# Attention results carried to the projection's input by transfers instead of transposes; projections evacuated by ScalarE and finished by GpSimd

## What is computed

```python
x = z; y = _layernorm(x)                        # 4 x 1024 x 256
zn = layernorm(y) * ln_scale + ln_bias;  q, k, v = zn @ w_qkv
att = softmax(q @ k.T / 4)                      # per head
out = (att @ v).reshape(b, n, 256) @ w_proj + b_proj
x = x + _layernorm(y + out)
x = x + _layernorm(ffn(_layernorm(x)))
# ffn: (ln(silu(t @ sw1.T + sb1) * (t @ sw2.T + sb2))) @ sw3.T + sb3; 512 rows of image 0 are routed
```

## Time and profile before

| | |
|---|---|
| median of 3 runs | 1050.6 us (1050.59 to 1052.78) |
| the profiled execution | 1052.78 us, span 1051.0 us |
| TensorE busy | 968.4 us, 92% |
| VectorE busy | 838.5 us, 80% |
| ScalarE busy | 606.2 us, 58% |
| GpSimd busy | 281.3 us, 27% |
| transfers | 49.4 MB |
| starts of the first and the last maxima reduction | 45.6 and 899.5 us |

### The profile page before, as it was taken

How to read it: one execution, slowest core, us unless ns; L and a number is a source line. 1 busy time by engine, 2 the same in 40 slices (tenths; PEclk the granted TensorE clock), 3 DMA queues, 4 the chain that set the end, 5 groups by cost and what they waited for, 6 DMA issues and landing times.

```text
span 1051.0 us, 16569 instructions
## 1 busy us (share of the span) xinstructions
PE 968.4 (92%) x6372; PEld 388.1 (37%) x6372; DVE 838.5 (80%) x1634; ACT 606.2 (58%) x700; POOL 281.3 (27%) x418
## 2 busy tenths in 40 slices
PE   4289999999999999999999999999999999966984
PEld 3123333333334334333343343333332333235773
DVE  4287888898887988999879889889899798445765
ACT  3025667677874775767857766667666666731110
POOL 4060001101622231207804412028142020633022
PEclk9697999999999999999999999999999999997998
DMA  5905101320160103200621031003410000231001
GB/s 139 134 1 69 54 2 41 53 70 2 41 93 30 60 22 46 69 9 1 109 94 41 1 45 52 27 1 71 91 60 24 1 2 1 78 133 52 1 1 60
DMA packets 45783, 49.42 MB, mean 47 GB/s; under 512 B 8409, under 2 KB 38889, under 8 KB 45321
## 3 DMA queue, kind: packets, MB, share of 16 engines
q1 hardware_dynamic: 44360, 46.53, 19.7%
q10 hardware_dynamic: 960, 0.79, 0.7%
q0 software_dynamic: 384, 1.05, 0.3%
HBM read 13.94 MB, written 8.91 MB: 22 GB/s over the span
## 4 chain that ended last, share of the span: by engine, by line
PE 83%; DVE 9%; DMA 2%; ACT 2%; issue 2%; POOL 1%; SPq 0%; ACTq 0%; DVEq 0%; POOLq 0%
PE obank L909 23%; PE sc L895 20%; PE ring L877 16%; PE ring L792 10%; PE ring L814 5%; DVE mx L1123 4%; PE sc L984 3%; PE ring L784 3%; PE ring L935 2%; DVE st L1059 2%; ACT prob L720 1%; DMA kp<-parts 1%; PE ring L929 1%; DMA qp<-mp 1%; DMA x_sb<-x 0%
## 5 line engine op out<-in xcount | busy, mean ns | idle before, releaser
L1123 DVE TENSOR_REDUCE mx<-ring 128x1 f32<-128x512 f32 x1024 | 635.1, 681 | 88.0 <-PE ring L877 86.3
L720 ACT ACTIVATE prob<-sc 128x1024 f32<-128x1024 f32 x512 | 495.9, 1021 | 205.4 <-PE sc L895 204.3
L877 PE MATMUL ring<-kp,qp 48*128 48x512 bf16 x1024 | 256.7, 390 | 31.7 <-issue 20.5
L895 PE MATMUL sc<-qp,kp 48*128 48x512 bf16 (+1 forms) x2048 | 274.2, 380 | 2.2 <-DMA qp<-mp 1.4
L909 PE MATMUL obank<-prob,vaug 128*32 128x512 f32 x2048 | 274.4, 608 | 0.7 <-ACT prob L720 0.7
L877 PEld LDWEIGHTS ring<-kp,qp 48*128 48x128 bf16 x1024 | 74.8, 93 | 275.4 <-DVE mx L1123 169.5
L895 PEld LDWEIGHTS sc<-qp,kp 48*128 48x128 bf16 (+1 forms) x2048 | 99.4, 95 | 105.4 <-ACT prob L720 20.0
L531 POOL TENSOR_TENSOR resid<-qkf,parts 128x1024 f32<-128x1024 f32 x8 | 17.1, 2132 | 207.7 <-ACT parts L668 207.7
L482 POOL TENSOR_TENSOR sum_m<-st 128x8 f32<-128x8 f32 x15 | 3.1, 209 | 257.3 <-DVE st L1059 257.3
L909 PEld LDWEIGHTS obank<-prob,vaug 128*32 128x32 f32 x2048 | 40.3, 108 | 65.1 <-issue 61.7
L537 POOL TENSOR_SCALAR parts<-resid 128x1024 bf16<-128x1024 f32 x14 | 14.7, 1050 | 181.2 <-DVE resid L1113 180.4
(11 more groups left out here) (190 smaller groups left out, 827.3 us busy)
## 6 DMA issues: line engine op xcount, KB each, us to landing
kp<-parts SPq DMA_DIRECT2D x96, 128.0 KB, 5.0
qp<-parts SPq DMA_DIRECT2D x180, 64.0 KB, 2.6
x_sb<-x SPq DMA_DIRECT2D x7, 1024.0 KB, 5.7
out<-hid SPq DMA_DIRECT2D x4, 1024.0 KB, 4.5
x_scratch<-x SPq DMA_DIRECT2D x3, 1024.0 KB, 4.7
qp<-mp SPq DMA_DIRECT2D x128, 2.0 KB
kp<-ew SPq DMA_DIRECT2D x1, 2048.0 KB, 8.2
x_sb<-x SPq DMA_DIRECT2D x2, 512.0 KB, 4.6
```

The costliest lines, as they stand in the source:

```text
L720: nc.scalar.activation(prob[:, e % 2, 2 * a:2 * a + 2, :].rearrange("p g n -> p (g n)"), sbuf2[a][:, :], ACT.Exp, scale=0.25).then_inc(s_f ...
L877: nc.tensor.matmul(dst[:, :], qp[rows, qh, h, qt * P:(qt + 1) * P], kp[rows, h, kh * HALF:(kh + 1) * HALF], start=True, stop=True).then_in ...
L895: ins = nc.tensor.matmul(dst[:, j * HALF:(j + 1) * HALF], kp[rows, h, kt * P:(kt + 1) * P], qp[rows, qh, h, :], start=plane == 0, stop=pla ...
L1123: nc.vector.tensor_reduce(mx[:, u % 2, n:n + 1], src[:, :], AX.X, ALU.max).then_inc(rv_free, 1)
```

## The change

- The "ot" and "a" items are gone, and with them VectorE's 32 reciprocals of 128x16 and products into `anat`. Instead, SyncE issues five transfers a unit (`result_rows`): one copies the four rows of sums to the 64 rows of `sums`, each sum row to the 16 rows of its head, and four copy the 16 result rows of a head to their place in `yA`, which has channels in rows. For the last unit two of them are ScalarE's.
- VectorE divides a 128x512 quarter of an image at a time (`divide`): a reciprocal of 128x512 of `sums`, a wait for it, and a product in place. Four such an image: at tau 41 and 47 for the first 8 heads, at tau 14 and 16 of the next image for the others; the last two of the 16 come after the loop.
- "p", "h" and "w" of images 0 to 2 are copied out of the ring by ScalarE, and GpSimd adds bias or x1 in SBUF one slot later.
- GpSimd makes the residual of one part (tau 40) that VectorE made at tau 44. A few items move by one to four slots. `pick` is made at the end of the loop instead of at the start.

```diff
-Z_AT = (14, 10)
-V_AT = (22, 25, 50, 51)
-P_AT = (20, 21, 23, 24)
+Z_AT = (14, 14)
+V_AT = (22, 25, 51, 52)
+P_AT = (19, 20, 21, 23)
-GATE_AT = (47, 48, 50, 51)
+D_AT = (41, 47, 14, 16)
+ROWS = 16 * (1 + GH)
...
-        if 1 <= w < B and 16 <= tau < 20:
-            fill.append(("a", w - 1, tau - 16))
-        if e >= 0 and e % 8 == 2 and 0 <= e // 8 - 1 < B * HU:
-            row.append(("ot", e // 8 - 1))
...
+ADDED = ("p", "h", "w")
+def by_act(key):
+    return key[0] in BY_ACT or key[0] in ADDED and key[1] < B - 1
...
+            def result_rows(u):
+                b, g, qh = u // HU, u % HU // NH, u % NH
+                n = 4 * b + 2 * (g // 2) + qh
+                row, cols = GH * HD * (g % 2), slice(qh * HALF, (qh + 1) * HALF)
+                sp.wait_ge(s_oT, u + 1)
+                if u % HU == 0 and b > 0:
+                    sp.wait_ge(r_full, R_INDEX["p", b - 1, 3] + 1)
+                if g % 2 == 0 and n >= 2:
+                    sp.wait_ge(s_div, n - 1)
+                sp.dma_start(sums[row:row + GH * HD, qh, :],
+                             oT[HD:P:VW, u % 2, :].rearrange("p (o n) -> p o n", o=1).to_broadcast([GH, HD, HALF]))\
+                  .then_inc(s_rows[qh], 16)
+                for i in range(GH if u < B * HU - 1 else GH // 2):
+                    sp.dma_start(yA[row + i * HD:row + (i + 1) * HD, g // 2, cols],
+                                 oT[i * VW:i * VW + HD, u % 2, :]).then_inc(s_rows[qh], 16)
...
+                for u in range(B * HU):
+                    if t == 8 * u + SL // HU + LEAD + (4 if u % HU == 0 else 1):
+                        result_rows(u)
...
+            def add(kind, b, i):
+                pool.wait_ge(ra_free, TAKEN[kind, b, i][1] + 1)
+                if kind == "p" and i == 0:
+                    pool.wait_ge(s_zb, b + 1)
+                t = slice(2 * i, 2 * i + 2)
+                if kind == "p":
+                    nc.gpsimd.tensor_tensor(x1[:, t, :], x1[:, t, :], zn[:, t, :], ALU.add).then_inc(s_added[kind], 1)
+                else:
...
+                if w + 1 < B and tau == 40:
+                    residual(w + 1, 1)
+                    split(w + 1, 1)
...
+                elif kind in ADDED:
+                    src = take_r(*key)
...
+                    dst = zn if kind == "p" else hid
+                    nc.scalar.activation(dst[:, 2 * key[2]:2 * key[2] + 2, :].rearrange("p t d -> p (t d)"), src[:, :],
+                                         ACT.Copy).then_inc(ra_free, 1)
...
                     sc.wait_ge(s_av, 8 * u + 8)
+                    if u >= NH:
+                        sc.wait_ge(s_rows[u % NH], ROWS * (u // NH))
                     nc.scalar.activation(oT[:, u % 2, :], obank[:, :], ACT.Copy).then_inc(s_oT, 1)
...
                 elif kind == "p":
+                    if key[2] == 0 or key[2] == 2 and b == B - 1:
+                        pe.wait_ge(s_div, 4 * b + (3 if key[2] == 0 and b == B - 1 else 4))
+                    project(key, yA, key[2], wp, KD)
...
+            def divide(b, kk, qh):
+                last_u = HU * b + (2 * kk + 1) * NH + qh
+                cols = slice(qh * HALF, (qh + 1) * HALF)
+                ve.wait_ge(s_rows[qh], ROWS * (last_u // NH + 1))
+                nc.vector.reciprocal(sums[:, qh, :], sums[:, qh, :]).then_inc(s_recip, 1)
+                ve.wait_ge(s_recip, 4 * b + 2 * kk + qh + 1)
+                nc.vector.tensor_tensor(yA[:, kk, cols], yA[:, kk, cols], sums[:, qh, :], ALU.mult).then_inc(s_div, 1)
...
+                if tau in D_AT:
+                    kk, qh = divmod(D_AT.index(tau), NH)
+                    if 0 <= w - kk and w < B:
+                        divide(w - kk, kk, qh)
...
             last = B - 1
             ve.wait_ge(s_wide, 1)
...
+            divide(last, 1, 0)
             for i in range(4):
                 h = i // 2
+                if i == 1:
+                    divide(last, 1, 1)
                 if i == 3:
                     normalize("y", last, x1, x1, 0, 4, D)
                 add_x1(last, i)
```

More of the change, by code:

```diff
@@ L76, in ring_order @@
             fill.append(("h", w - 1, H_AT.index(tau)))
[L77 to L80, removed]
+        if 1 <= w < B and 56 <= tau < 58:
+            fill.append(("u", w - 1, tau - 56))
+        if 1 <= w < B and 59 <= tau < 63:
+            fill.append(("w", w - 1, tau - 59))
         row = fill
@@ L85, in ring_order @@
             row.append(("mt", t // 8 - 1))
-        if e >= 0 and e % 8 == 2 and 0 <= e // 8 - 1 < B * HU:
-            row.append(("ot", e // 8 - 1))
         at[t] = row
     last = B - 1
-    at[SLOTS] = ([("a", last, i) for i in HALVES] + [("p", last, i) for i in range(4)]
+    at[SLOTS] = ([("p", last, i) for i in range(4)]
                  + [("x", last, 0), ("x", last, 2), ("h", last, 0), ("h", last, 1), ("x", last, 1), ("x", last, 3)]
@@ L149, in build @@
         hid = sb("hid", [P, NT, D])
-        anat = sb("anat", [P, NT, D])
+        yA = sb("yA", [P, KD, N])
+        sums = sb("sums", [P, NH, HALF])
         act = sb("act", [P, NT, F])
@@ L213, in build @@
         pickb = resid[:, HALF:N].bitcast(bf16).rearrange("p (e n) -> p e n", e=E)
-        xg, xgn = anat[:, 0:MT, :], anat[:, MT:2 * MT, :]
+        xg, xgn = (yA[:, i, :].rearrange("p (t d) -> p t d", d=D) for i in range(2))
+        pick = qkf[0:E, :].rearrange("p (e n) -> p e n", e=E)
         mhid = x_sb[:, 0:MT, :]
@@ L256, in build @@
         s_zb = sem("z_with_bias")
+        s_added = {k: sem("added_" + k) for k in ADDED}
         s_part = sem("first_part")
@@ L577, in _ @@
                     z_with_bias(w - 1)
+                if 1 <= w < B and tau - 1 in P_AT:
+                    add("p", w - 1, P_AT.index(tau - 1))
                 if 1 <= w < B and tau == 25:
@@ L584, in _ @@
                     nc.gpsimd.tensor_tensor(x1[:, :, :], x1[:, :, :], x_sb[:, :, :], ALU.add).then_inc(s_x1, 1)
-                if w + 1 < B and tau in (35, 44):
-                    split(w + 1, int(tau == 44))
+                if w + 1 < B and tau == 35:
+                    split(w + 1, 0)
                 if 1 <= w < B and tau == 36:
@@ L593, in _ @@
                     scaled(zn, x1, "x", 0, rstd["x"][:, 0, :], D).then_inc(s_norm["x"], 1)
-                if 1 <= w < B and tau == 51:
+                if w + 1 < B and tau == 40:
+                    residual(w + 1, 1)
+                    split(w + 1, 1)
+                if 1 <= w < B and tau - 1 in H_AT:
+                    add("h", w - 1, H_AT.index(tau - 1))
+                if 1 <= w < B and 60 <= tau < 64:
+                    add("w", w - 1, tau - 60)
+                if 1 <= w < B and tau == 52:
                     mean_of("u", w - 1, 0, F)
@@ L1214, in _ @@
                     i = F_AT[w == B].index(tau)
-                    for t2 in range(2):
-                        ve.wait_ge(rv_free, TAKEN["w", w - 2, 2 * i + t2][1] + 1)
+                    ve.wait_ge(s_added["w"], 4 * (w - 2) + 2 * i + 2)
                     if i == 0:
@@ L1252, in _ @@
                 for key in RING_AT[t]:
-                    if key[0] not in BY_ACT:
+                    if not by_act(key):
                         ring_item(key)
```

129 lines of the change are left out of this document (50 added, 79 removed).

## The result

The changed kernel takes **1113.1 us** (median), against 1050.6 for the kernel before on the same chip: a ratio of 1.0585, 95% interval 1.0561 to 1.0608. One of its four executions took 1813.5 us and is not in the ratio; why is not known, and the other three took 1110.6 to 1113.9. The kernel is slower by 62 us where 19 were forecast, and it lies outside the range given.

The account below looks back on a forecast made before the run. TensorE and VectorE were both taken as bounds, with 0.08 us slack in a plain slot. Loop 50.8 - 46.1 = 4.7 us longer plus end 14.6 made 19.3, giving 1070 us; range 1054 to 1087.

Parts of the forecast that it names:

- ot: Loop: removing the result transposes saves 26.6 us, 24 of them worth 1.01 each and six worth 0.39.
- the load stuck behind the rows: End: the last load of x goes out after the result rows, delaying GpSimd's pass; fourth add 15.2 us late.
- the reciprocal: VectorE's reciprocal of 128x512, extended from two smaller sizes at 6.6 ns an element: 3.52 us.
- The late rows: Loop, divides at tau 47: VectorE waits about 0.9 us each for rows still in transfer, 3.6 together.
- 4.15 less the slack of that slot: Loop: each divide holds VectorE 4.15 us and costs that minus its slot's slack; 50.8 us together with late rows.
- GpSimd ... so 0: Loop: GpSimd's added work, about 48 us, costs nothing, its products being wanted one or two slots later.
- the sum of what is removed: Loop: transposes, evacuations and residual taken off TensorE's and VectorE's slots save 46.1 us together.
- Evacuations and residual: Loop: evacuations moved to ScalarE save 6.7 and 4.6 us, the residual moved from VectorE to GpSimd 1.1.
- the slack of 0.67: Loop: seven divides beside a 0.59 us transpose have 0.67 us slack, so cost 3.48 each, 24.4 together.
- Rivals 1 and 2: Length of VectorE's reciprocal: first, 4.5 us, giving 1085, chance 0.20; second, cheap as a product, giving 1027, chance 0.09.
- rival 3: End: the late load of x does not hold it, giving 1056 us; chance 0.11.
- rival 4: Loop, divides at tau 47: the sums' transfer lands after 10 us, not 5, giving 1092; chance 0.07.

Follow-up runs that it names:

- e1_short: Changed kernel with each reciprocal on only 16 of its 512 columns, the division left out for the other 496; 1047.1 us, 0.9962 of the kernel before.
- e7_whole: Kernel before plus eight idle 64x512 reciprocals on VectorE, two an image in slots without a fill; 1099.2 us, ratio 1.0493.
- e3_bias: Changed kernel with GpSimd's bias add to x1 held until the divide at tau 16 is done, images 1 to 3; 1104.2 us, ratio 1.0498.
- e5_part: Kernel before with only ScalarE copying p, h and w, GpSimd adding, and GpSimd making the residual; transposes stay; 1044.7 us, ratio 0.9929.
- e9_dense: Changed kernel with 128x16 reciprocals except for the last four units, early load of x, bias add in four pieces, divides moved; 1037.1 us, ratio 0.9856.
- e4_split: Changed kernel with each loop reciprocal cut into four pieces of 128 columns over two slots, the product in the third; 1071.4 us, ratio 1.0202.
- e7_pieces: Kernel before plus eight idle 64x512 reciprocals, each cut into four pieces of 128 columns over two slots; 1093.6 us, ratio 1.0384.

## Why the prediction was right and wrong

Right was the sign and its reason: 16 long reciprocals on an engine without slack cost more than the transposes give back, and the load stuck behind the rows holds the end. Also right: the reciprocal (3.34 for 3.52, -2.5 us over 14) and most of the stopped slots themselves. They are 6.38 us at tau 41 of image 0 against 2.49 (+3.9; 4.07 was said), 6.39 against 3.07 beside an "x" (+3.3; 3.48), 6.50 against 4.41 beside an "h" (+2.1; 2.15). The late rows were 2.1 instead of 3.6.

**The step that failed is the price of a divide in the loop, "4.15 less the slack of that slot".** It ended with the stopped slot. The slots behind were taken as if TensorE went on at its old pace. Against the same slots of e1_short they are longer by 3.5, 5.3, 5.4 and 6.3 us in the four images, together **20.5 us** (a slot here runs from its first maxima reduction to that of the next; the slot behind tau 14 of image 2, where e1_short has a stop of its own, is set against 3.06). In image 0 the slots 41, 42, 43 behind the first divide are 3.05, 4.66 and 3.01, against 2.90, 2.47 and 2.49. They run at 1.2 GHz. That the stop is enough for this is shown by e7_whole, which has nothing else of the change.

The second failed step is "GpSimd ... so 0". It was priced by when its products are wanted, not by what it holds while it works: **8.4 us** from three products that stood for GpSimd. 8.0 of them are the bias add's, which e3_bias takes away; 0.4 is the residual's add in image 2.

The third is the sum of what is removed, too large by 6. "ot" was worth 0.90 and not 1.01, since the 2.61 us slot behind it has another cause and stays (580.90 - 578.29 in the changed kernel's bursts): 2.6. Evacuations and residual gave 7.0 in the profiled loop of e5_part where 12.4 was said: 5.4. Of these 2.0 are the slots at tau 25, which the changed kernel doesn't have (2.91 there), so 3.4 stay: "w" is 3.55, and the moved items cost something (the three slots from tau 49, with the value items, are 11.7 us instead of 11.3 an image).

A smaller error is in the slacks: the slots in which the divides at tau 14 of images 1 and 2 stand take 2.49 us in the kernel before, not 3.07, so the slack of 0.67 was not there: 1.2.

In sum 20.5 + 8.4 + 2.6 + 3.4 + 1.2 - 2.5 - 1.5 = 32.1 of the 36.1 us that the loop was missed by. Of the other 4.0, 2.6 are the clock's as well: 1.4 in slots 47 and 48 of image 0, which e1_short too has slowed (3.22 and 3.29 instead of 2.61 and 2.48), and 1.2 in the stopped slot at tau 16 of image 3, which begins at half clock. 0.7 is slot 28 of image 0, longer for a reason that was not looked for, and 0.7 stays unassigned. In the tail the chain up to the fourth add was off by 4.3 us, 1.5 of it in the issues, 0.9 in the landing and 1.9 in what follows the last divide, with the products at half clock; the whole tail was off by 3.3.

None of the rivals was the cause. Rivals 1 and 2 are excluded by 3343 ns, rival 3 by the 24.3 us wait, rival 4 by the 2.1 us. The repeat count of 8 that the Trainium skill gives the reciprocal (page "VectorE: DVE Perf Modes", section "First, the fixed hardware budget") had been read as the 4.5 us end; the measured 3.34 us decides for the slope. Both missing rivals can be had from the kind of row that was read. The kernel before has one fall of the clock in its loop, behind waits of 0.9 and 1.1 us, and a burst tells it (timeline of before):

```profile
796.55 1.06 PE L909 MATMUL obank<-prob,vaug 128*32 128x512 f32 x8
...
800.74 1.88 PE L909 MATMUL obank<-prob,vaug 128*32 128x512 f32 x8
```

The two slots behind it are 3.49 and 3.01 us where the changed kernel has 2.46 and 2.49: some 1.5 us for one fall. And the earlier trace rows showed a GpSimd add of 4.55 us whose place in the slots was not set against the divides.

What stays open: what exactly makes the clock fall (shown is only that it follows stretches in which TensorE stands, that the same short stops are sometimes followed by a fall and sometimes not, and that cutting a stop into pieces in bare slots doesn't always prevent it), why the early load is worth 20 us with whole reciprocals and 14 without, and the execution of 1813.5 us.

## What to carry to other kernels

When a change stops TensorE for microseconds in a full pipeline, price the slots behind the stop too: here a stop of 3 us or more cost another 1.5 to 1.8. Before an elementwise operation over a broadcast tensor goes to an engine without slack, look for the smallest layout of its distinct values: 2048 reciprocals as 128x16 took 0.24 us where 4096 of them, each repeated 16 times as 128x512, took 3.34, and two small transfers were cheaper than that. When work moves to GpSimd or beside it, list the VectorE operations with two SBUF inputs that can fall on any of GpSimd's adds, not only on the one that has been found: e9_dense moved one and still loses 6 us to another.

## What the runs showed of the hardware

- The reciprocal of VectorE takes 240 ns at 128x16 (e9_dense), 935 at 128x128 (e4_split) and 3343 at 128x512, so 6.2 to 6.3 ns an element a partition above the first 16; with half the partitions (64x512, e7_whole) it is 3349, the same.
- A VectorE product with two SBUF operands ended 0.55 us after the GpSimd add that it met, in all three images, whether it had met it at the start (4.98, 4.42) or near the end (1.12), and so in e1_short (2.40, 4.23, 0.98, 2.43) and e9_dense (4.51). Beside GpSimd's adds of 1.27 us it took 0.80. Beside a GpSimd operation on 128x8 it was not held (0.68, three times in e9_dense).
- TensorE fell to half clock after every stop of 3.0 to 7.3 us in the loops of the changed kernel (11) and e7_whole (8). After stops of 1.8 to 2.4 us it fell in e3_bias and not in the changed kernel, and after rows of stops of 0.6 to 1.0 us five times of eight in e7_pieces. It stayed there for 3 to 10 us, in the tail longer (41 us in the changed kernel, 17 before).
- SyncE needed 0.55 to 2.10 us to issue a row transfer in the changed kernel; five in a row took 4.5 us in the middle of the loop (196.28 to 200.83) and 5.7 at most.
